# Layer 1 recurrence: products k*v in PSUM, one PSUM buffer for the broadcast v, initial column written behind the product

## The reference

```
a = k_l[..., :, None] * v_l[..., None, :]
out = jnp.einsum('bhs,bhst->bht', r_l, faaaa * a + s)
s_new = a + w_l[..., None] * s
```

## Time and profile before

| | |
|---|---|
| median of 3 runs | 4331.4 us |
| lowest and highest run | 4328.8 and 4335.4 us |
| span of the profiled execution | 4338.2 us |
| TensorE, VectorE, ScalarE, GpSimd busy | 85%, 41%, 28%, 13% of the span |
| the recurrence's loop | from 995.7 to about 1247 us |

### The profile page before, as it was taken

One profiled execution on the slowest core, in us unless ns is written; L12 is line 12 of the kernel. 1 busy time (PEld: TensorE's weight loads), 2 busy tenths in 40 slices (PEclk: granted clock), 3 DMA queues, 4 the chain that ended last, 5 costly groups with the idle time before them and its releaser, 6 DMA issues. The chain is left out here.

```text
span 4338.2 us, 51209 instructions
## 1 busy us (share of the span) xinstructions
PE 3694.2 (85%) x17671; PEld 2781.4 (64%) x17671; DVE 1757.5 (41%) x3586; ACT 1221.5 (28%) x3084; POOL 559.9 (13%) x475
## 2 busy tenths in 40 slices
PE   4999979796658699999989789898989979688886
PEld 3777758453324487887878578787878867344442
DVE  2445442318873423323232422323232241566664
ACT  2344332111011123222222222222222232445452
POOL 0000020123430300000000100000000010432312
PEclk9999989899979799999999899999999989768688
DMA  2110120100000312222121132222122120110001
GB/s 85 48 46 25 37 77 15 38 10 3 0 10 29 106 42 78 74 59 80 41 73 46 38 109 55 84 55 84 41 78 55 27 80 10 61 38 27 31 2 31
DMA packets 142038, 209.09 MB, mean 48 GB/s; under 512 B 18915, under 2 KB 104357, under 8 KB 141933
## 3 DMA queue, kind: packets, MB, share of 16 engines
q0 software_dynamic: 67584, 94.64, 8.5%
q1 hardware_dynamic: 74348, 113.17, 8.5%
HBM read 191.04 MB, written 13.47 MB: 47 GB/s over the span
## 5 line engine op out<-in xcount | busy, mean ns | idle before, releaser
L63 PE MATMUL work<-cT_layer_hi,wk_layer_hi 128*128 128x362 f32 x1024 | 390.3, 381 | 0.0
L1908 ACT ACTIVATE p_layer<-scores,neg_max_layer 100x362 f32<-100x362 f32 x256 | 144.5, 565 | 740.4 <-DVE neg_max_layer L1963 739.1
L1944 DVE TENSOR_TENSOR values_layer<-work,value_bias_layer 121x512 f32<-121x512 f32 x192 | 132.4, 690 | 519.3 <-PE work L65 519.3
L64 PE MATMUL work<-cT_layer_lo,wk_layer_hi 128*128 128x362 f32 x1024 | 336.8, 329 | 0.0
L65 PE MATMUL work<-cT_layer_hi,wk_layer_lo 128*128 128x362 f32 x1024 | 336.6, 329 | 0.0
L63 PE MATMUL work<-wv_layer_hi,cT_layer_hi 128*121 128x512 f32 x768 | 311.9, 406 | 0.0
L64 PE MATMUL work<-wv_layer_lo,cT_layer_hi 128*121 128x512 f32 x768 | 303.1, 395 | 0.0
L65 PE MATMUL work<-wv_layer_hi,cT_layer_lo 128*121 128x512 f32 x768 | 302.6, 394 | 0.0
L1751 POOL DMA_DIRECT2D cT_layer_hi<-ctxT_hi x64 | 47.7, 745 | 1745.5 <-PE work L65 1743.3
L1890 ACT ACTIVATE keysT_layer<-work 128x361 f32<-128x361 f32 x256 | 120.7, 472 | 510.4 <-PE work L65 510.4
L1820 PE MATMUL o<-pT_layer,values_layer 121*128 121x100 f32 x1536 | 215.8, 276 | 56.9 <-ACT pT_layer L1914 56.9
(11 more groups left out here) (353 smaller groups left out, 7737.9 us busy)
## 6 DMA issues: line engine op xcount, KB each, us to landing
cT_layer_hi<-ctxT_hi POOLq DMA_DIRECT2D x64, 722.0 KB, 4.9
cT_layer_lo<-ctxT_lo POOLq DMA_DIRECT2D x64, 722.0 KB, 6.1
l0mlp_staged<-in_L_xattn_mlp_w_dram SPq DMA_DIRECT2D x16, 512.0 KB, 4.2
staged_layer<-in_L_xattn_wq_dram SPq DMA_DIRECT2D x8, 1024.0 KB, 5.2
staged_layer<-in_L_xattn_wk_dram SPq DMA_DIRECT2D x8, 1024.0 KB, 5.1
staged_layer<-in_L_xattn_wv_dram SPq DMA_DIRECT2D x8, 1024.0 KB, 5.1
staged_layer<-in_L_xattn_wo_dram SPq DMA_DIRECT2D x8, 1024.0 KB, 5.6
l2mlp_staged<-in_L_xattn_w_fc_dram SPq DMA_DIRECT2D x16, 512.0 KB, 4.1
```

Of the source, the lines that this page charges most:

```text
L63: pe.matmul(out, cut_a(a.hi), cut_b(b.hi), start=start, stop=False)
L64: pe.matmul(out, cut_a(a.hi), cut_b(b.lo), start=False, stop=False)
L1908: act.activation(probs[x % 4][:, 0:KEYS2], ps_scores[x % 2][0:L, 0:KEYS2], ACT.Exp, bias=neg_max[:, x:x + 1], accum_out=sums[:, x:x + 1]). ...
L1944: dve.tensor_tensor(values[c % 2][:, j, :], bank("v", c, j)[0:T2, :], value_bias[:, min(j, 1), :], ALU.add).then_inc(dve_copied, 1)
```

## The change

`kv` now lies in PSUM, two buffers of 1024 fp32 columns, that is two banks each. To make room for these four banks, `ps_v` has one buffer of two banks, so that all eight banks are taken (4 + 2 + 2). The waits follow: TensorE's broadcast t waits until product t - 1 is done (before: t - 2). ScalarE's copy of the start column waits until product t is done (before: scan t - 2), so it writes its two banks behind the product and not beside it. The scan reads the same 808 columns from PSUM. The order of the instructions on each engine, their number and their shapes stay as they were.

```diff
-        kv = [sb(f"kv{i}", [P, B, PREV]) for i in range(2)]
         state = [sb(f"state{i}", [P, B, PREV]) for i in range(2)]
...
-        ps_v = [own.enter_context(nc.psum_tensor(f"ps_v{i}", [P, HALVES, 512], F32)) for i in range(2)]
+        ps_v = own.enter_context(nc.psum_tensor("ps_v", [P, HALVES, 512], F32))
+        ps_kv = [own.enter_context(nc.psum_tensor(f"ps_kv{i}", [P, 1024], F32)) for i in range(2)]
+        kv = [t[:, 0:B * PREV].rearrange("p (b l) -> p b l", l=PREV) for t in ps_kv]
...
                         dve.tensor_tensor(
                             kv[t % 2][:, :, 1:PREV].rearrange("p (h b) l -> p h b l", h=HALVES),
-                            ps_v[t % 2][:, :, 0:HALF].rearrange("p h (b l) -> p h b l", l=L),
+                            ps_v[:, :, 0:HALF].rearrange("p h (b l) -> p h b l", l=L),
...
                         dve.tensor_tensor_scan(
                             state[u % 2][:].rearrange("p b l -> p (b l)"),
                             T["w"][:, bass.ds(m, 1), :, :].squeeze(1).rearrange("p b l -> p (b l)"),
-                            kv[u % 2][:].rearrange("p b l -> p (b l)"), 0.0, ALU.mult, ALU.add).then_inc(scanned, 1)
+                            ps_kv[u % 2][:, 0:B * PREV], 0.0, ALU.mult, ALU.add).then_inc(scanned, 1)
...
                 for t in range(N1):
-                    act.wait_ge(scanned, at(m, N1, t - 2))
+                    act.wait_ge(keyed, at(m, N1, t))
                     act.activation(kv[t % 2][:, :, 0], start[:, bass.ds(m, 1), :, t].squeeze(1), ACT.Copy
...
-                        pe.wait_ge(keyed, at(m, N1, t - 2))
+                        pe.wait_ge(keyed, at(m, N1, t - 1))
                         for part in (v.hi, v.lo):
                             for half in range(HALVES):
-                                mm = pe.matmul(ps_v[t % 2][:, half, 0:HALF], spread[:, t, :],
+                                mm = pe.matmul(ps_v[:, half, 0:HALF], spread[:, t, :],
```

## The result

The change makes the kernel faster: median 4275.3 us of 4 runs (4267.3 to 4292.5) against 4330.4 us of 4 runs of before. The ratio is 0.9881, with a 95% interval of 0.9852 to 0.9910, or 39 to 64 us less. The profiled execution has a span of 4265.6 us, 72.6 less than before, and where those 72.6 us come from is the first question.

What follows compares the result with a forecast made beforehand. VectorE was taken to bound the recurrence, with scans stretched beside GpSimd. Terms 39 - 6 + 9 - 1 = 41 us took the profiled 4338.2 to 4297, or 4290 us against the median 4331.4; range 4279 to 4308.

Steps and rivals of the forecast that it cites:

- The stretch: Recurrence mid-tile: scans with two SBUF inputs stand still beside GpSimd; kv in PSUM cuts steps 3.52 to 2.84, gaining 39 us.
- the stretch stays: Rival, chance 0.04: scan and GpSimd exclude each other for another reason, so scans stay long; about 4337 us.
- PSUM operands: VectorE's product and scan: kv in PSUM as output or input costs nothing; write bounded between 5 us gained and 10 lost.
- The rival of 20 us: Chance 0.08: PSUM on both sides is slow, each of 128 VectorE instructions pays the fixed part again; 4310 us.
- Single ps_v: One broadcast buffer: hidden under the scan in mid-tile with 0.57 us to spare, uncovered at tile starts; 6 us lost.
- The borders: Tile tails: GpSimd's last products no longer wait for scan 15, VectorE idles less; three tails of four undisturbed, 9 us gained.
- Lower clock early in a tile: Occurs once for some 3 us; there a step is TensorE's 4.0 us and the broadcast's cover is gone; 1 us lost.
- The rival on the slower side: Chance 0.03: TensorE becomes the bound, waits in every step with the clock at 1.2 GHz, steps of 4.0 us; 4369 us.
- no other stage changes: Outside the recurrence: every other stage keeps its time, so the recurrence's 41 us go into the kernel's time one for one.
- the 2 us of scatter: Allowance for scatter used in setting the low end of the range, 4279 us.

Runs made afterwards that it cites:

- waits-only kernel: Kernel before, kv still in SBUF, but with single ps_v, its broadcast waiting for product t-1 and the start column behind the product: 4332.3 us against 4327.0, ratio 1.0007.

## Why the prediction was right and wrong

**The stretch (forecast 39 us gained).** 155.6 - 116.5 = 39.1 us. Shown as a mechanism by three runs: the waits alone leave it, half the buffers in PSUM remove it in their half of the steps, and a shorter GpSimd product removes it with kv in SBUF. The rival "the stretch stays" falls with it.

**PSUM operands (forecast 0).** The product takes 1000 ns against 992, the scan the same as an unstretched one from SBUF. The start-to-start time from product to scan stayed at 0.90 to 0.91 us, so even the 8 ns do not show in the step. The 65 ns more for a PSUM source by the Trainium skill, "VectorE: DVE Perf Modes", are not seen here: 1826 ns from PSUM, 1829 from SBUF. The rival of 20 us falls.

**Single ps_v (forecast 6 us lost).** In mid-tile the broadcast is hidden, as said. At the starts, from product 0 to scan 0 is now 3.00 us (1046.40 to 1049.40) instead of 1.81, three times 1.19, and in the first tile some 1.7: 5.3 us. The loop of the waits-only kernel, which has the same starts, is 5.2 us longer as a whole.

**The borders (forecast 9 us gained).** VectorE's wait fell by 2.75 us at a border (7.20 to 4.45), 8 us for three, and in the last tile scan 15's end to yT's copy is 3.61 us (1195.35 to 1198.96) instead of 7.39, 3.8 more. 11.8 us: all four tails kept the full clock, where I had counted three.

**Lower clock early in a tile (forecast 1 us lost).** The price was near, but not the picture. "It occurs once for some 3 us" is a misreading of before already, where the second tile has a piece like the third's (granted clock 0.58 from 1065 to 1068 us). In the changed kernel it occurs in all four tiles, until 1008 us in the first and for some 10 to 12 us in each of the others. It stays cheap because most of it falls on steps without a gather, whose broadcast is hidden even at the lower clock; only the sixth product of each tile waits, 0.33, 0.44, 0.49 and 0.52 us, 1.8 in all. The sum of the measured terms is 39.1 - 5.3 + 11.8 - 1.8 = 43.8 us; the loops give 44.3. The forecast was 41. The rival on the slower side, TensorE as the bound at the lower clock, so began at every tile's start, but went no further: with gathers in TensorE's list from the fifth step on, the clock came back (1.00 from 1065 to 1086 us, for instance). (The terms of that rival add up to 4368 us, not 4369.)

**What failed is the step "no other stage changes" and the 2 us of scatter** that the range allowed with it. The three runs shown of before lay within 6.5 us and I took this for the scatter of the kernel. Layer 3's attention is not a fixed length: profiles of before have 532.1 and 538.7 us there, of the change 506.0, 513.1 and 532.2. With it the standard deviation of one run is 10 us, and a median of four is off by several us. From 4290 to 4275.3 are 14.7 us. 3.3 of them are the loop's, above all its undersized borders. 5.5 are scatter in the four runs of the change, whose median lies that much below their pooled mean, and 4.3 scatter in the start of the sum, 4331.4, which lies that much above the pooled mean of before. The rest, under 2 us, is within the standard error. The profile shows the same miss in one execution: 26.1 of its 72.6 us come from layer 3's attention, which was to stay as it was. The pooled mean of the change, 4280.8, lies inside the range; but for the scatter the forecast of the loop would have been good enough. A range of the same centre with the scatter in it, some 10 us more at either end, would have held.

**Left open:** what makes layer 3's attention take one course of the clock or another in the same program. The granted clock goes with its length (0.83 at 506, 0.81 at 513, 0.76 at 532), but which is the cause was not tried, nor can 46.2 against 44.3 us, with a standard error of 3.0, exclude a mean gain there of up to some 8 us.

## To carry to other kernels

If a VectorE instruction with two SBUF inputs is longer beside a GpSimd instruction than alone, look for one operand that can lie in PSUM: the scan here then ran beside GpSimd, at the speed that it has alone. What pays for the PSUM banks is a single buffer elsewhere, and here that cost only where there was no other work to cover it, at the starts of a tile; writing the loop through its borders took that back too. And before a range is set, ask which stages run with a changing clock: three runs that agree do not show the scatter of a kernel, and a profile difference is to be split by stage before any of it is credited to the change.

## What was not expected

- ScalarE's copy of 8 elements takes 186 ns into PSUM and 218 ns into SBUF, in one kernel.
- One program's runs spread over 42 us (4305.4 to 4347.6, 70 runs), and most of it comes from one stage of 532 us; without layer 3 four runs lie within 4.4 us.
- A tail of matmuls in which TensorE pauses 1.2 us at most kept the granted clock at 1.00 in all four tiles, and one whose longest pause was 1.9 to 3.4 us lost it in each. Yet right behind the first kind, with a pause of 1.1 to 1.3 us at every broadcast, the clock fell to 0.50 each time.
